# Attention steps of a two-layer macaron block: probabilities normalised ahead of their transposes, the values product turned round

## The reference

```python
def local_attention(q, k, v):          # 8 heads of 64; windows of 64 tokens
    bq = q.reshape(b, h, w, WINDOW, d) * QK_SCALE
    bk, bv = (look_around(bk), look_around(bv))     # previous and own window: 128 keys
    sim = jnp.einsum('bhwid,bhwjd->bhwij', bq, bk)
    mask = (i < j) | (i > j + WINDOW) | (j == -1)
    sim = jnp.where(mask, -jnp.finfo(sim.dtype).max, sim)
    attn = jax.nn.softmax(sim, axis=-1)
    return jnp.einsum('bhwij,bhwjd->bhwid', attn, bv)

def _layer(x, ...):                    # twice per F
    q, k, v = split(shift_token(x) @ wqkv)
    q, k = rotary_xpos(l2norm(q) * qs, l2norm(k) * ksc)
    x = x + local_attention(q, k, v) @ wo
    h = layernorm(shift_token(x)) * lg + lb
    a, g = split(h @ w1 + b1)
    return x + (a * gelu(g)) @ w2 + b2
```

## Time and profile before

| | |
|---|---|
| median of 3 runs | 1258.79 us |
| profiled execution, its own time | 1265.98 us |
| its span, first to last instruction | 1264.2 us |
| mean granted TensorE clock | 0.919 of full |
| PE busy | 1030.9 us (82%) |
| DVE busy | 739.5 us (58%) |
| ACT busy | 681.2 us (54%) |
| POOL busy | 527.6 us (42%) |
| run 0 of F, about | 22 to 376 us |
| run 1 of F, about | 485 to 870 us |

### The profile page before, as it was taken

One profiled execution on the slowest core, in us unless ns is written; L12 is line 12 of the kernel. 1 busy time (PEld: TensorE's weight loads), 2 busy tenths in 40 slices (PEclk: granted clock), 3 DMA queues, 4 the chain that ended last, 5 costly groups with the idle time before them and its releaser, 6 DMA issues. The chain is left out here.

```text
span 1264.2 us, 25908 instructions
## 1 busy us (share of the span) xinstructions
PE 1030.9 (82%) x9078; PEld 635.6 (50%) x9078; DVE 739.5 (58%) x1625; ACT 681.2 (54%) x1292; POOL 527.6 (42%) x405
## 2 busy tenths in 40 slices
PE   5789999999998686899999999987149976814995
PEld 1445555555553282555555555533139952414885
DVE  2577777767684463777676767753814426571442
ACT  4567667667646615665755766534126635503561
POOL 2675455554422532554444443400645510074441
PEclk9899999999999878999999999998569987956998
DMA  9895334454337002544444443303112230011223
GB/s 337 265 307 117 87 88 99 102 135 98 90 78 100 1 3 63 124 110 92 102 102 102 98 97 89 90 18 150 42 51 65 65 92 0 18 46 51 56 65 117
DMA packets 88943, 120.57 MB, mean 95 GB/s; under 512 B 20368, under 2 KB 72336, under 8 KB 87920
## 3 DMA queue, kind: packets, MB, share of 16 engines
q1 hardware_dynamic: 82256, 96.84, 32.1%
q0 software_dynamic: 6272, 20.44, 4.4%
q10 hardware_dynamic: 288, 1.63, 0.3%
HBM read 63.21 MB, written 22.11 MB: 67 GB/s over the span
## 5 line engine op out<-in xcount | busy, mean ns | idle before, releaser
L1691 POOL TENSOR_TENSOR arena<-arena 128x1024 f32<-128x1024 f32 x64 | 150.9, 2357 | 325.2 <-DVE arena L1318 321.9
L1680 POOL TENSOR_TENSOR arena<-arena 128x1024 f32<-128x1024 f32 x64 | 150.9, 2358 | 51.0 <-ACT arena L999 51.0
L552 PE MATMUL banks<-arena 128*128 128x512 f32 x256 | 126.2, 617 | 14.8 <-ACT arena L999 8.6
L1663 POOL DMA_INDIRECT moe_rows<-arena x64 | 64.8, 1012 | 170.6 <-DVE arena L1516 152.0
L991 ACT ACTIVATE arena<-banks,arena 128x512 f32<-128x512 f32 x128 | 80.8, 681 | 97.0 <-PE banks L627 96.6
L1310 DVE TENSOR_REDUCE arena<-banks 128x4 f32<-128x512 f32 x128 | 82.6, 688 | 79.9 <-PE banks L580 79.2
L1670 POOL DMA_INDIRECT moe_outs<-arena x78 | 81.5, 1045 | 103.6 <-DVE arena L1580 58.4
L1172 ACT ACTIVATE arena<-banks,arena 128x128 f32<-128x128 f32 x312 | 89.0, 369 | 61.9 <-PE banks L843 59.7
L1318 DVE TENSOR_TENSOR arena<-arena 128x1024 f32<-128x1024 f32 x64 | 78.2, 1222 | 25.5 <-DMA arena<-arena 25.3
L1004 ACT ACTIVATE arena<-banks 128x1024 f32<-128x1024 f32 x64 | 65.7, 1026 | 50.3 <-PE banks L552 49.5
L853 PE MATMUL banks<-arena 128*128 x624 | 86.6, 282 | 5.5 <-ACT arena L1172 4.8
(11 more groups left out here) (199 smaller groups left out, 1986.2 us busy)
## 6 DMA issues: line engine op xcount, KB each, us to landing
arena<-arena SPq DMA_DIRECT2D x256, 128.0 KB, 3.8
arena<-rstd SPq DMA_DIRECT2D x128, 256.0 KB, 4.3
moe_rows<-arena POOLq DMA_DIRECT2D x12, 903.0 KB, 7.1
arena<-moe_rows SPq DMA_DIRECT2D x78, 64.5 KB
arena<-in_rot SPq DMA_DIRECT2D x4, 1024.0 KB, 11.5
arena<-in_mw SPq DMA_DIRECT2D x2, 2048.0 KB, 11.3
arena<-moe_outs SPq DMA_DIRECT2D x16, 256.0 KB, 5.1
arena<-ssm_a SPq DMA_DIRECT2D x4, 512.0 KB, 5.8
```

The lines of the kernel that those rows point to most:

```text
L552: mm(bank[k], w_qkv[d][:, w0:w0 + P], src, start=True, stop=True).then_inc(proj, 1)
L1680: nc.gpsimd.tensor_tensor(TA[:, n % 2], RAW, ROTV[:, :, 0, c * C:(c + 1) * C], ALU.mult).then_inc(cos_done, 1)
L1691: nc.gpsimd.tensor_tensor(TA[:, n % 2], TA[:, n % 2], TB, ALU.add).then_inc(rot_sum, 1)
```

## The change

The softmax is finished before the transposes. In round n+2 ACT takes the exponentials from banks 3 and 4 itself, in eight pieces of 128 columns, with the negated row maximum as bias (`scores_exp`); DVE sums them and takes the reciprocal (`sums`); POOL multiplies (`divide`). In round n+3 PE transposes the probabilities into banks 5 and 6, DVE copies them out (`copy_scores`), and `values` has V as stationary and the probabilities as moving operand, so that the result comes out with features on partitions; ACT copies it to `OT`, which has five slots for four. `transpose_out`, `subtract`, the old `divide` and the column of ones go. Half of V is emptied by DVE. The parts of `gate` and `hidden` are spread from the head of the hp-1 round. Of the first layer norm only chunk 0 stands ahead of the rounds; the others are in rounds 1, 4 and 5. In S the exponentials of the decays come behind the norms, the scan is in four pieces, and the sums on `X` are spread.

```diff
@@ tensor engine
-                def transpose_out(s, n, at):
-                    pe.wait_ge(o_norm, 2 * n + 2)
-                    bank7_read(pe, run, at)
-                    for t in range(TILES):
-                        last = nc.tensor.transpose(bank[7][:, t * P:(t + 1) * P], ON[:, n % 2, t], ident)
-                    last.then_inc(ot_mm, 1)
...
+                def values(s, n):
+                    hp, gg = s % HP, 2 * NCH * run + s // HP
+                    pe.wait_ge(pt_evac, 2 * n + 2)
+                    if hp == 0:
+                        pe.wait_ge(v_carry, gg + 1)
+                        pe.wait_ge(v_shift, 4 * gg + 4)
+                    for w in range(2 * TILES):
+                        for e in range(2):
+                            last = mm(bank[5][e * DH:(e + 1) * DH, w * WIN:(w + 1) * WIN],
+                                      (VS if w % 2 == 0 else V)[:, w // 2, 2 * hp + e, :], PRT[:, e, w * WIN:(w + 1) * WIN],
+                                      start=True, stop=True)
+                    last.then_inc(o_mm, 1)
...
+                def transpose_scores(s, n, e):
+                    pe.wait_ge(p_norm, 2 * n + e + 1)
...
+                        last = nc.tensor.transpose(bank[5 + e][:, t * P:(t + 1) * P], PR[:, e, t * P:(t + 1) * P], ident)
+                    last.then_inc(pt_mm, 1)
@@ scalar engine
-                        act.wait_ge(pt_mm, 2 * n + e + 1)
-                        after(act, o_mm, 2 * (n - 1) + e + 1)
-                        A(PRT[:, e], bank[3 + e][:], ACT.Exp, bias=zero_c).then_inc(pt_evac, 1)
...
+                def scores_exp(n, e):
+                    act.wait_ge(s_max, 2 * n + e + 1)
+                    after(act, pt_mm, 2 * (n - 1) + e + 1)
+                    for t in range(TILES):
+                        last = A(PR[:, e, t * P:(t + 1) * P], bank[3 + e][:, t * P:(t + 1) * P], ACT.Exp, bias=mx[:, e, t:t + 1])
+                    last.then_inc(p_exp, 1)
...
             def ssm():
...
-                decays_exp(1)
-                decays_exp(2)
                 ssm_square(3, 0)
...
+                for q in range(2, 8):
+                    decays_exp(q)
@@ vector engine
-                        TT(by_row(PR[:, e]), by_row(bank[3 + e][:]), wide(mx[:, e], P), ALU.subtract).then_inc(s_sub, 1)
...
+                def copy_scores(n, e):
+                    dve.wait_ge(pt_mm, 2 * n + e + 1)
+                    after(dve, o_mm, n)
+                    nc.vector.tensor_copy(PRT[:, e], bank[5 + e][:]).then_inc(pt_evac, 1)
+
+                def sums(n, e):
+                    dve.wait_ge(p_exp, 2 * n + e + 1)
+                    nc.vector.tensor_reduce(total[:, e], by_row(PR[:, e]), AX.X, ALU.add).then_inc(p_sum, 1)
+                    dve.wait_ge(p_sum, 2 * n + e + 1)
+                    nc.vector.reciprocal(rec[:, e], total[:, e]).then_inc(p_rec, 1)
+
+                def carry_v(g, gg):
...
+                    nc.vector.tensor_copy(VS[WIN:P, 0], V[WIN:P, TILES - 1]).then_inc(v_carry, 1)
...
+                if kind == "F":
+                    norm_chunks(norm0, shifted, [0])
@@ gpsimd
+            def divide(n):
+                by_row = lambda a: a.rearrange("p (t k) -> p t k", t=TILES)
+                for e in range(2):
+                    pool.wait_ge(p_rec, 2 * n + e + 1)
+                    nc.gpsimd.tensor_tensor(by_row(PR[:, e]), by_row(PR[:, e]), rec[:, e].unsqueeze(2).to_broadcast([P, TILES, P]),
+                                            ALU.mult).then_inc(p_norm, 1)
...
                     if s < STEPS:
                         cosine(s, STEPS * run + s)
+                    if s >= 2:
+                        divide(STEPS * run + s - 2)
```

More of the change, by code:

```diff
@@ L44 @@
 MB = MH // P
-VW = DH + 1
+VW = DH
 NT = 2 * T // P + NE - 1
@@ L583, in scores @@
                     last.then_inc(s_mm, 1)
[L585 to L597 removed]
+                def values(s, n):
[10 more added lines that the diff above has]
+                    last.then_inc(o_mm, 1)
                 def square_sum(s, n):
                     pe.wait_ge(sq_done, n + 1)
[L601 removed]
+                    if s % HP == 1 and s // HP >= 2:
+                        pe.wait_ge(gl_done, 3 * (2 * NCH * run + s // HP - 1))
+                    else:
+                        bank2_read(pe, run, s)
                     for j in range(4):
@@ L696, in ffn @@
                     n, hp, g = STEPS * run + s, s % HP, s // HP
+                    mlp = 0 <= g - 2 < 2 * NCH
+                    gating = mlp and hp == 1
+                    if gating:
+                        hidden(g - 2, s, 0)
                     if s < STEPS:
                         project(s, n)
-                    if 0 <= s - 4 < STEPS:
-                        transpose_out(s - 4, n - 4, s)
+                    if s in LN_STEP:
+                        first_centred(norm0, LN_STEP[s], run, s)
+                    if mlp and hp == 0:
+                        mlp_centred(g - 2, s)
+                    if gating:
+                        hidden(g - 2, s, 1)
                     if run == 0 and s == STEPS + 3:
+                        pe.wait_ge(ot_evac, STEPS)
                         ssm_variance(0, 0)
@@ L903, in _ @@
             for k, (kind, norm0, run) in enumerate(plan):
-                cen_bank[0] = 4 * (kind == "F" and run)
                 if kind in "MU":
@@ L946, in ssm_input, with state_decays @@
                   ACT.Copy).then_inc(u_evac, 1)
-            def state_decays(k):
+            def state_decays(k, parts):
                 act.wait_ge(e_in[k], 32)
-                for z in range(2):
+                for z in parts:
                     v = flat(E[k])[:, 2 * C * z:2 * C * (z + 1)]
@@ L973, in norm_root @@
                 need(act, ln_rstd, n0 + (c - 1))
-                A(lt[:, c % 2], bank[4 - cen_bank[0] + c][:], ACT.Ln, bias=eps_c).then_inc(ln_log, 1)
+                A(lt[:, c % 2], bank[4 + c][:], ACT.Ln, bias=eps_c).then_inc(ln_log, 1)
                 need(act, ln_log, n0 + (c + 1))
@@ L1049, in mlp_norm @@
                     act.wait_ge(mn_var, gg + 1)
-                    A(MLT, bank[2][:], ACT.Ln, bias=eps_c).then_inc(mn_log, 1)
+                    A(MLT, bank[6 if s < STEPS else 2][:], ACT.Ln, bias=eps_c).then_inc(mn_log, 1)
                     act.wait_ge(mn_log, gg + 1)
                     A(MLT, MLT, ACT.Exp, scale=-0.5, bias=zero_c).then_inc(mn_rstd, 1)
-                act.wait_ge(pool_init, 3 * (run + 1))
+                act.wait_ge(pool_init, 2 * (run + 1))
                 for s in range(ROUNDS):
@@ L1737, in _ @@
                 nc.gpsimd.memset(V, 0.0).then_inc(pool_init, 1)
-                pool.wait_ge(pool_init, 3 * run + 2)
-                nc.gpsimd.memset(V[:, :, :, DH:VW], 1.0).then_inc(pool_init, 1)
-                for s in range(STEPS + 1):
-                    if s:
+                for s in range(STEPS + 2):
+                    if 1 <= s <= STEPS:
                         rotated(s - 1, STEPS * run + s - 1)
```

438 lines of the change are left out of this document (235 added, 203 removed).

## The result

The changed kernel takes 1370.22 us (median of 4 runs, 1366.36 to 1372.71) against 1260.84 for the kernel before beside it: ratio 1.086, 95% interval [1.083, 1.090]. The forecast was 1345, range 1235 to 1400, slower with 0.74. The profiled execution took 1372.71 us with a span of 1370.9.

The account below looks back on a forecast made before the run. PE was taken to set the time, busy 43.02 of 44.21 us a period. +69 +30 -13 = +86 on the profiled 1265.98 gave 1352, or 1345 us against the median; range 1235 to 1400.

Parts of the forecast that it names:

- The period: Four attention steps laid out through all engines: 50.9 us against 44.2, taken as +6 for sliding.
- C: DVE's `copy_scores` in each step: 1.25 us; `values` waits for it, 1.35 after scores.
- The port: Port shared by VectorE and GpSimd locks for whole instructions: period 50.9 us with the lock, 45.5 without.
- N: DVE's `normalise` in each step, with two SBUF inputs: mean about 1.0 us, well above 0.71.
- D: POOL's new `divide`, two 128x512 products a step: costed at 1.15 us each, expected near 1.2 in the profile.
- lock-free rival: No lock worth the name between DVE and POOL: period 45.5 us, total 1264; chance 12%.
- PE stays the bound: Rival: DVE and POOL end up hidden under PE, period 39.4 us, total 1183; chance 18%.
- Steps 8 to 31: Attention steps with the MLP beside them, both runs: 11.5 periods at +6 us, +69.
- Steps 0 to 8: Eight steps ahead of the MLP, bounded by POOL plus `normalise` and `rotate` at 9.6 us: +15 a run.
- The clock: Rival: PE idles so long that its clock falls, +58 us over the periods, total about 1400; chance 10%.
- Outside: Edits outside the steps: later norm chunks -5 us, decay exponentials -6, scan in four pieces -2; -13 in all.
- behind them I take 0: Rounds behind steps 8 to 31 of each run: no added time, 0 us.

Follow-up runs that it names:

- e11: Kernel before, with timed meetings of single VectorE operations and a GpSimd product behind its last store; an SBUF copy went from 0.43 to 2.26 us.
- e3: Changed kernel with `carry_v`'s copy of 64x512 on ACT instead of DVE; 1365.2 us, ratio 1.081.
- e1: Changed kernel with POOL's two `divide` products a step left out, so the probabilities stay unnormalised; 1334.6 us, ratio 1.056.
- e5: Changed kernel with the softmax sums written by ACT's accumulator output, DVE taking only the reciprocal; 1350.5 us, ratio 1.070.
- e6: Changed kernel with sums by ACT's accumulator, `divide` on DVE instead of POOL, and `carry_v` on ACT; 1343.2 us, ratio 1.066.
- e12: Changed kernel with `values` moved behind the MLP's last product and the output product in every fourth round (hp 3); 1353.5 us, ratio 1.071.
- e2: Changed kernel with the two `divide` products on DVE behind its reciprocal, none on POOL; 1387.5 us, ratio 1.098.
- e4: Changed kernel without the state-space table pieces in run 0, that layer getting a table of zeros; 1368.0 us, ratio 1.081.

## Why the prediction was right, and where its sizes were off

- *The period.* Laid out: 14.1, 8.7, 14.1, 14.0, with sliding 50.2; measured 13.72, 8.16, 13.86, 14.33, sum 50.06. (The terms of the first add up to 13.9, not 14.1; that changes nothing here.) The steps hold one by one: `values` waits 1.23 for C (1.35 said), HN to the gate products stays long (PE waits 30.7 us for it in all, and from the variance matmul to HN's end it takes 3.9 again, 778.48 to 782.41), but not because POOL holds the port: HN takes 0.55 us in all sixteen rounds, before and after, and stands behind ACT's two activations on the variance as before; `carry_v` and one shift a half are blocked.
- *The port.* Shown directly by e11. In a period at full clock `carry_v` loses 2.15, N's second operation 0.84 twice, a shift copy about 0.3 twice: 4.4 us of blocked DVE, for 5.5 in the prediction; N's two means average 0.93 (1.0 said), `carry_v` 2.32 (2.5), D 1.13 (1.2). But blocked time isn't period time: e3 gave 1.33 back for 2.15 and e1 1.74 for 2.3. The lock-free rival's 45.5 would need both and 1.5 more; e1 and e3 added give 47.0, and no run made both edits. So the lock is about half of the loss of 5.9 at most (e1 also takes D's own length away, and e5 and e6 show that gains in hp 2 don't simply add). The wait for C, 1.14 by e12, and S, up to 1.6 in hp 2 by e5, belong to the chain itself. That the sum of the layout came out within 0.2 us doesn't show each of its terms.
- *PE stays the bound.* False: PE idles 8 of 50 us. DVE's sum of work isn't the bound of a period either, only that of hp 2 to 3 (e2). PE is busy 84% of the period, not 78%: I had taken its work from start to start, the busy time counts overlapped and stretched instructions.
- *Steps 8 to 31*, +69: measured +33.8 in run 1 (34.5 said) and +44.1 in run 0. The 10 too much go with run 0's table pieces: 10.8 by e4. Part of that is the clock, whose share in these steps (the sum below) fell from 11.3 to 3.4 us with the pieces left out. In the prediction the pieces stood nowhere.
- *Steps 0 to 8*, +15 a run: measured +14.9 and +18.5. POOL's relief in e1 gives 6 of them back, not all: POOL's occupation was part of the reason, not the bound that I named.
- *The clock.* The trace was read in slices of 3.5 us, and (1 - granted clock) x length was added up: 14.2 us in run 0 and 6.9 in run 1, against 1.7 each before. The fall priced in e3 cost 1.53 us and counts 1.7 in this sum. At that price the 17.7 more are some ten falls and about 16 us (an estimate), which lie in the items above. The falls behind the last steps (below) come on top of the sum. I had the clock as a rival of +58 at 10%; it is a part of the result, of smaller size.
- *Outside.* -13 said, -4.7 measured, and the small number hides three larger ones. The edits themselves gave nearly what was said. First projection of run 1: 5.9 behind the start of its first norm product, 11.8 before, so -5.9 (-5 said). The scan: from the first state matmul to the last read's end 20.5 before and 18.9 now, -1.6 (-2 said). The exponentials: from the start of the last output product of run 0 to the first state matmul 50.7 before and 46.5 now, -4.2 (6 said). The step that failed is "behind them I take 0". The last step of each run has nothing beside it, and the longer softmax stands bare; in run 0:

```profile
440.12 1.10 PE L589 MATMUL banks<-arena 64*64 64x128 f32 x32
...
445.27 2.15 PE L642 MATMUL banks<-arena 128*128 128x128 f32 x8 [2.76 <-POOL arena L1775]
448.21 1.98 PE L602 MATMUL banks<-arena 128*64 128x64 f32 x32 [0.79 <-DVE arena L1373]
```

Behind the wait of 2.76 us the granted clock stood at its lower level; this window starts with the transposes at 445.27 (columns as in the earlier trace rows):

```profile
445.27:450.12 4.85, 4.06 (x41) 3.22 (x41) 1.39 (x2) 0.00 (x0) 0.98 (x1) 0.50 0.31 83
```

From the start of the last N's second operation to the last output product it takes 23.6 us for 17.9 in run 0 and 20.6 for 15.4 in run 1, +5.7 and +5.2, at a mean clock of 0.83 in both for 1.00 before: the waits for D and C, and the clock that fell behind them. In run 1, +4.4 of it are left at the mixture's first matmul of 8 columns, and the stages behind that, whose work the change doesn't touch, took 3.6 less in this execution (383.3 for 386.9; over the other profiled executions they took 379 to 390). That is luck, and it hid the second tail. By the sign that I had set, a stretch between the two runs of steps shorter by some 8 us, the smaller part is wrong: it is shorter by 5.8 (121.3 for 127.1 from N to N). And the restart, answering:

```profile
532.23 1.13 PE L532 MATMUL banks<-arena 128*128 128x512 f32 x2 [0.82 <-DVE arena L1538]
534.05 1.13 PE L538 MATMUL banks<-arena 128*128 128x512 f32 x2 [0.69 <-ACT arena L948]
538.13 3.78 PE L568 MATMUL banks<-arena 128*128 128x512 f32 x4 [2.96 <-DVE arena L1341]
```

Sum on the profiled executions: +14.9 +18.5 +77.9 -4.7 = +106.6 (the spans differ by 106.7), for +86 predicted. The 20 us too few are about 10 in run 0's steps and 8 in the item outside.

Open: how the loss divides between the lock and the longer chain (no run takes the lock away alone), and what decides whether the clock falls in one period and not in the next.

## What to carry to other kernels

Lay out each round as a chain through all engines, from one fixed event to the next, and count a moved operation where it stands in that chain: here the totals of all engines were laid out at under 40 us and measured at up to 42, and the period was 50. Ask it interval by interval: over the whole period DVE has 8 us to spare, in one of the four intervals none. Where DVE and GpSimd share a stage, ask of each DVE operation whether it has two SBUF inputs or is a one-input copy or `tensor_scalar` in SBUF; sums, and whatever has an input in PSUM, may stand beside GpSimd, the others wait for its whole instruction. Behind a product that must wait for a copy, put work that waits for nothing, and look at the ends of loops, where a longer chain has no cover.

## What the hardware showed that I had not expected

- An accumulator output of ACT costs an instruction of 0.21 us each (e5), over half of the 128-column exponential that it serves (0.37).
- A copy or `tensor_scalar` of 512 fp32 columns within SBUF takes 0.43 us, a sum or a product from SBUF 0.69, a copy from PSUM or a product with one input there 0.68. GpSimd blocked the two quick ones and the product with two SBUF inputs; the sum and the two with an input in PSUM it left alone (e11).
- The granted clock fell to its lower level more often in the changed kernel (21.1 us by the sum above, for 3.4 before), and one fall cost 1.53 us (e3). Ahead of it PE had waited 1.12 and 1.23 us; in another round, with waits of 1.03 and 1.23, nothing fell.
